# One order planned anew: eight-bit rounding of weights placed elsewhere, parts of q and k written four times, another block order

## What is computed

```python
x = x + _L0_attn_ref(_layernorm(x))   # one head of 64, causal
x = x + _L0_ffn_ref(_layernorm(x))    # x and weight rounded to float8_e4m3, x @ w.T + bias
x = x + _L1_attn_ref(_layernorm(x))   # 16 heads of 16, rope on q and k, causal
x = x + _L1_ffn_ref(_layernorm(x))    # sigmoid(xr Wr) * (relu(xk Wk)^2 Wv)
```

## Time and profile before

| | |
|---|---|
| median of three runs | 2739.94 us (2739.13 to 2746.29) |
| the profiled execution, whole | 2741.72 us |
| its span, first to last instruction | 2739.8 us |
| PE busy | 2477.3 us (90%) |
| DVE busy | 1998.2 us (73%) |
| ACT busy | 1555.1 us (57%) |
| POOL busy | 596.8 us (22%) |
| mean granted clock of PE | 0.964 |
| DMA | 176.09 MB, 64 GB/s over the span |

### The profile page before, as it was taken

One profiled execution on the slowest core, in us unless ns is written; L12 is line 12 of the kernel. 1 busy time (PEld: TensorE's weight loads), 2 busy tenths in 40 slices (PEclk: granted clock), 3 DMA queues, 4 the chain that ended last, 5 costly groups with the idle time before them and its releaser, 6 DMA issues.

```text
span 2739.8 us, 57369 instructions
## 1 busy us (share of the span) xinstructions
PE 2477.3 (90%) x21618; PEld 1129.0 (41%) x21618; DVE 1998.2 (73%) x4256; ACT 1555.1 (57%) x2785; POOL 596.8 (22%) x584
## 2 busy tenths in 40 slices
PE   5788789999999999999989999899999989999996
PEld 3444233433444444343434434343344433433344
DVE  4666688787877687768876687877777769888822
ACT  2234456576655556556655556556565656666662
POOL 4544120303114121221303313031222310000011
PEclk8899899999999999999999999999999999999998
DMA  1433222121311313030221312213031131111110
GB/s 44 115 99 102 86 76 59 48 86 41 98 40 44 109 46 101 25 110 25 70 72 42 96 53 81 61 46 104 17 108 38 36 110 54 40 50 42 30 39 28
DMA packets 238911, 176.09 MB, mean 64 GB/s; under 512 B 88752, under 2 KB 238384, under 8 KB 238640
## 3 DMA queue, kind: packets, MB, share of 16 engines
q1 hardware_dynamic: 237872, 171.51, 21.9%
q10 hardware_dynamic: 768, 0.92, 0.1%
HBM read 87.36 MB, written 84.41 MB: 63 GB/s over the span
## 4 chain that ended last, share of the span: by engine, by line
PE 57%; DVE 21%; SPq 7%; ACT 6%; issue 4%; DMA 3%; POOL 1%; DVEq 1%; POOLq 0%; ACTq 0%
PE psum L1721 13%; DVE mx L1421 13%; PE psum L1698 11%; PE psum L1669 6%; SPq L852 4%; PE psum L1637 4%; ACT probs L1196 3%; PE psum L1601 2%; PE psum L1572 2%; PE psum L1511 2%; PE psum L1752 2%; PE psum L1741 2%; PE psum L1772 2%; PE psum L1656 2%; PE psum L1760 2%
## 5 line engine op out<-in xcount | busy, mean ns | idle before, releaser
L1196 ACT ACTIVATE probs<-psum 128x512 f32<-128x512 f32 x2176 | 1143.8, 604 | 627.8 <-PE psum L1698 398.2
L1421 DVE TENSOR_REDUCE mx<-psum 128x1 f32<-128x512 f32 (+2 forms) x2304 | 1289.3, 622 | 260.8 <-PE psum L1669 167.5
L1698 PE MATMUL psum<-qst,kst 34*128 34x512 bf16 (+7 forms) x5120 | 667.6, 352 | 51.8 <-ACT probs L1196 15.5
L1721 PE MATMUL psum<-probs,vs 128*17 128x512 f32 (+3 forms) x5120 | 595.5, 547 | 1.8 <-ACT probs L1196 0.9
L1669 PE MATMUL psum<-kst,qst 64*128 64x512 bf16 (+3 forms) x2560 | 438.8, 356 | 88.1 <-DMA qst<-rest_dram 29.3
L1698 PEld LDWEIGHTS psum<-qst,kst 64*128 64x128 bf16 (+1 forms) x5120 | 195.1, 95 | 395.0 <-DVE mx L1421 122.7
L1669 PEld LDWEIGHTS psum<-kst,qst 64*128 64x128 bf16 x2560 | 133.0, 94 | 415.6 <-ACT probs L1196 149.9
L1721 PEld LDWEIGHTS psum<-probs,vs 128*17 128x17 f32 x5120 | 93.3, 96 | 195.9 <-issue 162.5
L990 POOL TENSOR_SCALAR vare<-mv 128x4 f32<-128x4 f32 x64 | 15.3, 238 | 657.1 <-DVE mv L1298 657.1
L1146 ACT ACTIVATE probs<-psum 128x1024 f32<-128x1024 f32 x80 | 74.9, 940 | 109.5 <-PE psum L1586 54.1
L1676 PE MATMUL psum<-maskq,identh 64*128 64x64 bf16 (+1 forms) x2048 | 128.6, 206 | 0.0
(11 more groups left out here) (160 smaller groups left out, 2848.8 us busy)
## 6 DMA issues: line engine op xcount, KB each, us to landing
main_dram<-parts SPq DMA_DIRECT2D x224, 128.0 KB
qst<-main_dram SPq DMA_DIRECT2D x128, 128.0 KB, 2.7
kst<-main_dram SPq DMA_DIRECT2D x128, 128.0 KB, 2.8
rest_dram<-parts SPq DMA_DIRECT2D x112, 128.0 KB
v_dram<-vst SPq DMA_DIRECT2D x64, 136.0 KB, 3.9
vs<-v_dram SPq DMA_DIRECT2D x64, 136.0 KB, 2.2
xs<-x_in SPq DMA_DIRECT2D x16, 512.0 KB, 4.0
x_dram<-xs SPq DMA_DIRECT2D x16, 512.0 KB, 3.0
```

Source lines behind the costliest of these rows:

```text
L1196: act.activation(dst, src, ACT.Exp, scale=DK1 ** -0.5).then_inc(S["exp"], 1)
L1421: ins = dve.tensor_reduce(mx1[:, n % 2, 2 * g + odd, tile % TPC, c:c + 1], bank(src, at, at + cols), AX.X, ALU.max)
L1698: ins = pe.matmul(two[odd][:, at:at + cols], kst[rows, kslot, part, pair, keys], qst[rows, qslot, part, pair, CH - cols:CH], start=(part = ...
L1721: ins = pe.matmul(bank(7, off, CH, rows=VW, row=32 * h), vtile[:, h, :], probs[:, HG * (step_no(b, hg, k) % 2) + h, at:at + CH - off], sta ...
```

## The change

1. `eight_bit_weights` becomes a job `wf8` of DVE, right behind the first norm of chunk (0, 0); `FFN` waits for that job.
2. The three parts are stored in four slices, not six: `STORED` is hi, mid, lo, hi for q and hi, mid, hi, lo for k. One tensor `qk_dram` takes them. The same six products are formed: a load reads slices 0 and 1, then again 0 and 1 (q) or 1 and 2 (k), then 2 and 3. A `put` is four DMAs in place of six. A load is six DMAs of 32 partitions and 64 KB in place of four.
3. Blocks are q half 0, k half 0, q half 1, k half 1: `half, side = divmod(bl, 2)`. Head groups 0 and 1 need blocks 0 and 1 only.
4. SP issues wo0 behind x of chunk 1; wf has a semaphore of its own, apart from bf.
5. POOL builds the masks behind `root` of chunk 0, and its kst memsets begin one `root` earlier.
6. In the planner the load of x of chunk (0, 1) has a latency of 9.0 in place of 4.0, `put` one of 5.0 in place of 6.0, `bias0` comes after `turnmax0 d` of (0, 0), and `PATIENCE` is 0.25 in place of 0.2. All lists of all engines are made anew from this.

```diff
-TERMS = [(0, 0), (0, 1), (1, 0), (1, 1), (0, 2), (2, 0)]
-MAIN = 4
+STORED = ((0, 1, 2, 0), (0, 1, 0, 2))
+PAIRED = ((0, 0), (0, 1))
...
-PATIENCE = 0.2
+PATIENCE = 0.25
...
+    if c == (0, 0):
+        add("DVE", "wf8", c, key(), 6.5, ("norm", (0, *c)))
...
-                (wo0[0:DK0, 0:D], w["wo0"]), (wo0[DK0:P, 0:D], w["wo0"]),
...
             load_x(0, 1)
+            for rows in (slice(0, DK0), slice(DK0, P)):
+                sp.dma_start(wo0[rows, 0:D], w["wo0"]).then_inc(S["weights"], 16)
...
-                    side, half = divmod(bl, 2)
+                    half, side = divmod(bl, 2)
                     wt.job("lo", item)
-                    for n, term in enumerate(TERMS):
-                        to, at = (main_dram, n) if n < MAIN else (rest_dram, n - MAIN)
-                        rows = to[b, side, 8 * half:8 * (half + 1), at, :, CH * q:CH * (q + 1)]
-                        sp.dma_start(rows, split(b, bl)[:, term[side], :]).then_inc(S[f"put {bl}"], 16)
+                    for n, part in enumerate(STORED[side]):
+                        rows = qk_dram[b, side, 8 * half:8 * (half + 1), n, :, CH * q:CH * (q + 1)]
+                        sp.dma_start(rows, split(b, bl)[:, part, :]).then_inc(S[f"put {bl}"], 16)
...
-                        sp.dma_start(into[HALF * odd:HALF * (odd + 1), slot, 0, :, :],
-                                     main_dram[b, side, heads, :, :, cols].rearrange("g n d t -> (n d) g t")
-                                     ).then_inc(loaded, 16)
-                        sp.dma_start(into[HALF * odd:HALF * odd + REST, slot, 1, :, :],
-                                     rest_dram[b, side, heads, :, :, cols].rearrange("g n d t -> (n d) g t")
-                                     ).then_inc(loaded, 16)
+                        of = qk_dram[b, side, heads, :, :, cols].rearrange("g n d t -> n d g t")
+                        for part, row, first in [(0, 0, PAIRED[side][0]), (0, REST, PAIRED[side][1]), (1, 0, 2)]:
+                            row += HALF * odd
+                            sp.dma_start(into[row:row + REST, slot, part, :, :],
+                                         of[first:first + 2, :, :, :].rearrange("n d g t -> (n d) g t")
+                                         ).then_inc(loaded, 16)
...
-                    if item == (0, 0, 1):
+                    if item == (0, 0, 0):
                         masks(n)
...
-                        eight_bit_weights()
```

More of the change, by code:

```diff
@@ L340, in both @@
         return (("turned", (ln, *c)),)
-    add("SP", "load x", c, key() - (60.0 if b else 1e4), 0.1, ("store x2", p2), ("norm", p2 and (2, *p2)), lat=4.0)
+    add("SP", "load x", c, key() - (60.0 if b else 1e4), 0.1, ("store x2", p2), ("norm", p2 and (2, *p2)), lat=9.0 if c == (0, 1) else 4.0)
     norm(0, ("load x", c))
@@ L345, in chunk_jobs @@
     last = same and ("scores0", (*same, TPC * (same[1] + 1) // 2 - 1))
-    add("POOL", "bias0", c, key(0), 2.4, ("norm", (0, *c)))
+    add("POOL", "bias0", c, key(0), 2.4, ("norm", (0, *c)), ("turnmax0 d", (0, 0)))
+    if c == (0, 0):
+        add("DVE", "wf8", c, key(), 6.5, ("norm", (0, *c)))
     add("PE", "QK0", c, key(), 1.71, *both(0), lat=0.1, claim="P", mode="F")
@@ L392, in chunk_jobs @@
     add("POOL", "bias", c, key(), 2.4, ("norm", (1, *c)))
-    add("PE", "FFN", c, key(), 0.9, *both(1), lat=0.1, claim="D", mode="F")
+    add("PE", "FFN", c, key(), 0.9, *both(1), ("wf8", (0, 0)), lat=0.1, claim="D", mode="F")
     add("ACT", "ffn", c, key(), 0.93, ("FFN", c), *[("addf", p and (*p, n)) for n in range(2)], free=("FFN", c))
@@ L416, in chunk_jobs @@
         add("POOL", "lo", (*c, bl), key(0.3), 1.12, ("mid", (*c, bl)))
-        add("SP", "put", (*c, bl), key(0.3), 0.6, ("lo", (*c, bl)), lat=6.0)
+        add("SP", "put", (*c, bl), key(0.3), 0.6, ("lo", (*c, bl)), lat=5.0)
     for n in range(2):
@@ L430, in head_jobs @@
         slot = block_before(b, hg, q, KRING)
-        add("SP", "load k", me, pos - LEAD - 25, 0.4, ("put", (b, q, 2 + hg // 2)),
+        add("SP", "load k", me, pos - LEAD - 25, 0.4, ("put", (b, q, 2 * (hg // 2) + 1)),
             *(scored_with(*slot) if slot else []), lat=4.5)
         slot = block_before(b, hg, q, QRING)
-        add("SP", "load q", me, pos - LEAD - 25, 0.4, ("put", (b, q, hg // 2)),
+        add("SP", "load q", me, pos - LEAD - 25, 0.4, ("put", (b, q, 2 * (hg // 2))),
             *(scored_for(*slot) if slot else []), lat=4.5)
@@ L721, in build @@
         att_dram = nc.dram_tensor("att_dram", [B, T, D], F32, kind="Internal").ap()
-        main_dram = nc.dram_tensor("main_dram", [B, 2, H, MAIN, DK1, T], BF16, kind="Internal").ap()
-        rest_dram = nc.dram_tensor("rest_dram", [B, 2, H, len(TERMS) - MAIN, DK1, T], BF16, kind="Internal").ap()
+        qk_dram = nc.dram_tensor("qk_dram", [B, 2, H, len(STORED[0]), DK1, T], BF16, kind="Internal").ap()
         v_dram = nc.dram_tensor("v_dram", [B, NHG, P, NT, HG * VW], F32, kind="Internal").ap()
-        names = KINDS + ["weights", "weights f", "weights r", "weights q", "weights later", "const", "ready", "ready later", "chain d", "chain p",
+        names = KINDS + ["weights", "weights f", "weights b", "weights r", "weights q", "weights later", "const", "ready", "ready later", "chain d", "chain p",
                          "chain s", "spread", "apart"]
@@ L751, in parts_put @@
         def parts_put(wt, b, q, bl):
-            wt.wait_ge(f"put {bl}", 16 * len(TERMS) * (chunk_no(b, q) + 1))
+            wt.wait_ge(f"put {bl}", 16 * len(STORED[0]) * (chunk_no(b, q) + 1))
         def v_put(wt, b, q):
@@ L1029, in _ @@
                     b, q = item
-                    wt.wait_ge("weights f", 32)
+                    wt.wait_ge("weights b", 16)
                     wt.job("norm", (1, b, q))
@@ L1255, in eight_bit_weights @@
                 low, high = wf8[:, 0:2 * D], wf8[:, 2 * D:4 * D]
-                wt.wait_ge("weights f", 32)
+                wt.wait_ge("weights f", 16)
                 dve.tensor_tensor(pick, raw, raw, ALU.mult)
@@ L1622, in _ @@
                     b, q = item
-                    wt.wait_ge("ready", 2)
+                    wt.job("wf8", (0, 0))
                     turned(wt, 1, b, q)
```

20 lines of the change are left out of this document (12 added, 8 removed).

## The result

The changed kernel takes 2668.9 us in the median (2668.14 to 2672.76) against 2740.4 of the kernel before: 0.9738 of its time, 95% interval 0.9721 to 0.9755, 71 us less. The forecast was 2719, with 2701 to 2738 as its range. The sign was right, and the size was wrong by 50 us.

The account below looks back on a forecast made before the run. Behind the ramp a full queue with PE 93% busy, in the ramp latency; 13.6 + 2.5 + 3 + 5 - 3 = 21.1 us less than 2741.72, 2720.6, and 1.8 less against the median: 2719 us, range 2701 to 2738.

Parts of the forecast that it names:

- The reading order: Windows first: behind the ramp a queue, PE 93% busy, at most 180 us idle for good; then the ramp's timeline, as latency.
- Writes and loads elsewhere: SP's queue outside the ramp: 32 DMAs fewer and 64 more per batch, a loss of 3 us.
- The six loads as the price: Rival, SP's queue behind the ramp: six loads for four are slower, 2751 us; chance 0.11, shared with the new lists.
- The opening, 13.6 us: Start of the ramp: earlier first norm and hidden rounding bring `scores0` of chunk 0 from 43.25 to about 29.6, 13.6 us.
- the lead is lost on the way: Rival, ramp: the first 16 us are gone before 310, only the end of the ramp remains, 2735 us; chance 0.17.
- The rounding: On DVE in the opening: takes 5.4 us without POOL, in place of 9.62, and is hidden, ending at 19.4.
- The rival on it: Rounding not hidden, met by POOL or wf late: opening gains 9.4 in place of 13.6, 2723 us; chance 0.10.
- The clock, 2.5 us: PE behind the 10.87 us stall that ends at 43.25: the 0.50 clock goes too, 2.5 us, between 0 and 5.
- Maxima of chunk 2: In the ramp: they no longer go out behind a block's writes, 3 us, between 0 and 4.25.
- end of the ramp: q of chunk 3 loaded 10 us earlier, scores of chunk 2 about 14 later: 5 us, between 0 and 10.
- New lists: Behind the ramp all lists differ in small ways: left at 0, with 8 us allowed both ways.
- The test that it named: Wrong if chunk 3's first write isn't at least 15 us earlier, or is and the total isn't: then PE's idle grew.

Follow-up runs that it names:

- four_old_lists: The kernel before with the new storage alone (four writes of a block, six loads of 32 partitions), all lists as before: 2695.7 us, 0.9834.
- opening_alone: The kernel before with only points 1, 4, 5 and, of point 6, x's latency and `bias0`'s place; lists made anew: 2744.1 us, 0.9994.
- the added writes: Changed kernel, same job order, two more writes per block into a tensor nobody reads: 2727.7 us, 0.9944; with 32 of 512 columns 2706.2 us, 0.9874.

## Why the prediction was wrong, point by point

**The reading order misled.** The forecast took the stretch behind 320 us as a queue that is full, "what is idle for good is at most 180 us". It is full to 93%, but the idle time in it isn't for good. It fell to 148.7 us there. The middle, at 93% as well, still had 49.5 us to give, about half of them in busy time, and that is more than the ramp gave.

**"Writes and loads elsewhere": a loss of 3 us, between a loss of 6.2 and a gain of 5. This step failed.** It is the term of the sum that was mis-sized: the storage gives 45 us on the old lists and 59 on the new. Four things went into it:

- Fewer writes were priced at one block's two issues, 1.24 us, for four waits, 5 us at the best. But the load that PE waits for at 917.87 stood behind two blocks, twelve writes in a row, and SP gained 3.1 us ahead of it. On the lists of before, the five waits for q behind the ramp fell from 24.6 to 15.6 us where the forecast had them grow by up to 6.2. In the ramp, PE's waits for q went from 4.8 to 0 and those for k from 8.6 to 4.5; k was not in the price at all.
- The waits that hang on a write were not looked up: ACT's `hi` for its slot of `parts`, then DVE's `res`, then PE for the maxima. In the trace they bear the names of the last engine in the chain. On the lists of before ACT's fell from 16.8 to 3.9 us and DVE's behind them from 42.2 to 30.9.
- Two loads more were to cost 1.24 us. Six loads of 32 partitions took SP 0.427 us each in the median, against 0.588 to 0.617 for the four old ones, those of 32 partitions too, so that a set of six took 2.67 to 3.35 us in the ramp where the forecast's 0.62 gave 3.7.
- The clock was priced once, behind the stall at 43 us, and not for the many short stalls of the middle. Of the 46.7 us between the profiled spans of the kernel before and `four_old_lists` it made up 19.5.

**The six loads as the price.** The forecast had 0.11 on a slower kernel from them or from the new lists, and weighed a rule of the Trainium skill for it (DMA: Bandwidth & Descriptors, section "Rules for kernel authors"): transfers to partition halves run one after the other, one over all partitions is better. The earlier trace rows show only that half the bytes land nearly as late; that one transfer waits for the other they don't show. Here the six narrow loads beside six writes gave 0.9944 against 0.9969 of the four, so to split these loads further, which are waited for seldom, costs nothing in the time. Neither kernel makes the one transfer that the rule advises, so the rule itself was not tried.

**The opening, 13.6 us.** Right at its marks (9.98 and 29.65), and 14 us in the changed kernel; but its reason to reach the end was wrong. "a microsecond taken out of the ramp's chain should come out of the total nearly whole" is refuted by `opening_alone`: 24.7 us at the first output, none at the end. The rival "the lead is lost on the way" described this, and the place: with the opening alone the first write of chunk 3 is 0.5 us early. It is lost only in some lists. That the changed kernel keeps it is luck as far as the forecast goes, which had nothing to tell the lists apart.

**The rounding.** Hidden, as forecast, and without the 2.45 and 2.56 us of the earlier trace rows; POOL's write of `kst` met it in one instruction and cost 0.7 us, which nobody waited for. The rival on it is out.

**The clock, 2.5 us.** The stall at 43 us shrank from 10.87 to 3.36 us, but the window is still at 0.66, and the one from 60 to 70 at 0.56. PE's busy time up to the fourth output is the same as before (335.05 and 334.93 us), so that term was nearer to 0. The clock as a whole gave 19 us of PE's busy time, elsewhere.

**Maxima of chunk 2 and end of the ramp, 3 and 5 us.** The maxima go out at 118.35 in place of 142.20 and the first write of chunk 3 at 260.97 in place of 286.51. At the fourth output the lead is 26.4 us, against 24.1 of the forecast's terms without the loads and writes. The sum fits, the parts can't be told apart: `four_old_lists` gains 17.7 us up to the same mark with no new opening at all, so the ramp's gain has two sources that don't add. The fit is partly luck: with the old patience alone the first write of chunk 3 goes at 278.56, 17.6 us later, and what the changed lists give there was in no term of the sum.

**New lists, 0 within 8 us.** Too narrow. With storage and opening in all of them, five lists came to 0.9752 (two of them), 0.9793, 0.9836 and 0.9843 of the time before, which is 25 us from the best to the worst.

**The test that it named** said that if the first write of chunk 3 was early, the ramp was right. It was, by 25.5 us. For a wrong total it looked only for more idle time behind the ramp, not for less.

## What to carry to other kernels

Before a DMA is priced at what the bounding engine waits for it, count the whole burst of issues that stands ahead of a waited-for load on its queue, and follow the buffer that the DMA reads: who may not overwrite it until it has landed, and who stands in a fixed list behind that one. Here two blocks are written back to back, and taking a third of the writes out of the burst was worth 53 us with loads and lists unchanged; moving issues earlier where nobody waits gave nothing. A stretch that is 93% busy can still hold a gain, since short stalls of PE can cost clock too. A lead won at the start is kept by some lists and lost by others; in the list that lost it here, it had gone into scores and values, and the maxima were left with little beside them.

## What was not expected of the hardware

- The time that a DMA's issue takes on SP differs from one access to the next, and neither bytes nor partitions alone set it. Medians: 0.57 us for 128 KB from 128 partitions into slices of `qk_dram`, and 0.47 for the added writes from as many partitions into a plain tensor, with the full bytes as with a sixteenth of them; 0.59 to 0.62 for an old load to 64 partitions, 0.59 for an old one to 32, 0.43 for a new one to 32. GpSimd took 0.60 us for the same write that takes SP 0.57.
- A sixteenth of the bytes in the two added writes saved a third of their cost (0.9944 to 0.9874); the other two thirds stayed.
- Behind a stall of 2.58 us the clock fell to 0.50 for some 4 us, after PE had begun to work again. Of what the storage alone gave, 46.7 us in the profiled spans, 19.5 are the clock.
